# Channel attention: the bounds of the scores made from the queries' signs by GpSimd and TensorE, the key scans read from PSUM, and the own queries' work moved by a step

## The reference

```
Q = (x @ Wq + bq).reshape(b, s, H, C) * inv_sqrt_c      # H = 16 heads, C = 64 channels
K = (x @ Wk + bk).reshape(b, s, H, C)
V = (x @ Wv + bv).reshape(b, s, H, C)
scores = jnp.einsum('bshq,bshk->bshqk', Q, K)           # an outer product of 64 queries and 64 keys
scores = jnp.where(triu(ones((C, C)), 1), -inf, scores)  # channel q sees the keys 0..q
w = jax.nn.softmax(scores, axis=-1)
attn = jnp.einsum('bshqk,bshk->bshq', w, V).reshape(b, s, HID) @ Wo + bo
```

## Time and profile before

| | |
|---|---|
| median of 3 runs | 3225.54 us (3220.49 to 3230.01) |
| the profiled execution's own time | 3221.55 us |
| its span, first to last instruction | 3217.70 us |
| busy: TensorE / VectorE / ScalarE / GpSimd | 2606.6 / 2244.1 / 1852.5 / 1556.9 us |
| granted TensorE clock, mean | 0.946 |
| first scans of the four batches of the channel stage | 1525.29, 1927.99, 2330.64, 2733.28 us |
| exponentials of the own queries (L1660) | 2048, in all 708.2 us |

### The profile page before, as it was taken

One profiled execution on the slowest core, in us unless ns is written; L12 is line 12 of the kernel. 1 busy time (PEld: TensorE's weight loads), 2 busy tenths in 40 slices (PEclk: granted clock), 3 DMA queues, 4 the chain that ended last, 5 costly groups with the idle time before them and its releaser, 6 DMA issues. The chain is left out here.

```text
span 3217.7 us, 52070 instructions
## 1 busy us (share of the span) xinstructions
PE 2606.6 (81%) x19172; PEld 2068.6 (64%) x19172; DVE 2244.1 (70%) x4214; ACT 1852.5 (58%) x4363; POOL 1556.9 (48%) x1473
## 2 busy tenths in 40 slices
PE   1998799889987998777688876888768887688867
PEld 0465556555655565577577766777667776677757
DVE  2167516751675168523999969999699996999964
ACT  0364536453645355422877748777487774877743
POOL 0141314131413142312987729877298772987725
PEclk8999999989998999888999998999989999899988
DMA  9400000000000000075000000000000000000005
GB/s 239 130 2 1 5 10 2 1 5 10 2 1 5 10 2 1 18 274 185 4 8 1 1 4 4 7 1 1 4 4 7 1 1 4 4 7 1 1 28 161
DMA packets 75363, 93.12 MB, mean 29 GB/s; under 512 B 9325, under 2 KB 61340, under 8 KB 74985
## 3 DMA queue, kind: packets, MB, share of 16 engines
q1 hardware_dynamic: 24388, 51.54, 4.9%
q10 hardware_dynamic: 45540, 27.93, 3.6%
q0 software_dynamic: 5184, 10.29, 1.0%
HBM read 61.58 MB, written 28.62 MB: 28 GB/s over the span
## 5 line engine op out<-in xcount | busy, mean ns | idle before, releaser
L1701 POOL TENSOR_TENSOR arena<-arena 128x1536 f32<-128x1536 f32 (+9 forms) x480 | 1035.7, 2185 | 293.1 <-DVE arena L1765 247.7
L1569 PE MATMUL psum<-ident,arena 128*128 128x128 f32 (+7 forms) x7168 | 880.6, 282 | 293.3 <-ACT arena L1670 286.2
L1569 PEld LDWEIGHTS psum<-ident,arena 128*128 128x128 f32 (+7 forms) x7168 | 806.9, 139 | 397.5 <-ACT arena L1670 351.1
L1660 ACT ACTIVATE arena<-arena 128x64 f32<-128x64 f32 (+7 forms) x2048 | 708.2, 485 | 122.0 <-PE psum L1578 122.0
L1765 DVE TENSOR_TENSOR arena<-arena,psum 128x1536 f32<-128x1536 f32 (+9 forms) x480 | 494.7, 1064 | 52.8 <-ACT arena L1670 45.1
L1670 ACT ACTIVATE arena<-arena 128x1536 f32<-128x1536 f32 (+2 forms) x288 | 406.7, 1416 | 177.5 <-DVE arena L1751 177.5
L901 POOL TENSOR_SCALAR arena<-arena 128x512 f32<-128x512 f32 (+3 forms) x512 | 263.9, 532 | 498.5 <-DVE arena L864 498.3
L1751 DVE TENSOR_TENSOR arena<-arena,psum 128x1536 f32<-128x1536 f32 (+9 forms) x480 | 493.8, 1063 | 14.3 <-POOL arena L1701 12.5
L822 ACT ACTIVATE arena<-arena 128x512 f32<-128x512 f32 (+3 forms) x512 | 281.8, 552 | 183.2 <-DVE arena L857 183.2
L518 POOL TENSOR_SCALAR veps<-mv 128x1 f32<-128x1 f32 x112 | 21.5, 192 | 615.2 <-DVE mv L513 610.5
L775 PEld LDWEIGHTS psum<-ident,arena 128*128 128x128 f32 x1280 | 142.4, 145 | 169.9 <-ACT arena L833 84.7
(11 more groups left out here) (274 smaller groups left out, 3619.2 us busy)
## 6 DMA issues: line engine op xcount, KB each, us to landing
arena<-in_L_ffn_W SPq DMA_DIRECT2D x39, 768.0 KB
arena<-in_L_ffn_W SPq DMA_DIRECT2D x23, 514.0 KB
rows_d<-xrow ACTq DMA_DIRECT2D x1, 9504.0 KB, 51.0
y_d<-xrow ACTq DMA_DIRECT2D x1, 9216.0 KB
arena<-rows_d SPq DMA_DIRECT2D x62, 66.0 KB
y_d<-arena POOLq DMA_DIRECT2D x39, 64.0 KB
arena<-in_L_ffn_h_w ACTq DMA_DIRECT2D x2, 1024.0 KB
wa<-in_L_attn_W_attn ACTq DMA_DIRECT2D x1, 1536.0 KB
```

The lines of the kernel that those rows point to most:

```text
L1569: last = nc.tensor.matmul(ps[ch.half][0:rows, to:to + P], buf[:, c:c + rows], ident[:], start=first, stop=False, is_transpose=True, skip_g ...
L1660: nc.scalar.activation(by_key[:, 0:HD - r, j], keys[:, h, 0:HD - r], ACT.Exp, bias=NB[:, j:j + 1], scale=Q3[tt % 2][:, j:j + 1]).then_inc( ...
L1701: last = nc.gpsimd.tensor_tensor(of_piece(D3[n % 5], piece), q, keys_on(K3[tt % 2], k, nk, w), ALU.mult)
```

## The change

- Ahead of the tiles a matrix `minus` (the negative identity) is made once.
- `move_qk` also writes the queries' positive and negative parts (`QS`, two Relu, one with scale -1) for each half, and the keys by head a second time, into `psK`, the PSUM banks 5 and 6. The two scans read psK instead of KH, at step 11 instead of 12. The banks of psD are swapped.
- `maxima` is gone from VectorE, and ScalarE's copy of the queries into psM too. GpSimd multiplies the positive part by the maxima and the negative part by the minima (`times_pool`, four products of 128x512 a tile, and NB), at its steps 16 and 0; TensorE subtracts the one from the other into psM with two matmuls (`bound_pe`), at step 14 for one half and step 0 for the other.
- The own queries' shares lie in steps 2 to 13; their denominators' sums in steps 14 and 15, their weighing in 15 and 16, their numerators' sums in 16 and 17, ahead of the V fill of step 17.
- At a batch's start GpSimd does this behind the products of the chunks 0 and 1.

```diff
-        psD = [psum[:, 6, :], psum[:, 7, :]]
+        psD = [psum[:, 7, :], psum[:, 6, :]]
+        psK = psum[:, 5:7, :].rearrange("p a n -> p (a n)")
...
-        Q0_AT, MAX_0, FINISH_0, V1_AT = NC - 1, 0, 3, 3
+        FINISH_0, V1_AT = 3, 3
...
-        SCAN, MAX_1 = EARLY + 6, EARLY + 8
+        SCAN, TIMES_1, BOUND_1 = EARLY + 5, NC - 2, NC - 4
+        TIMES_0, BOUND_0 = 0, 0
...
-        OWN_STEPS = range(1, NC - 3)
+        OWN_STEPS = range(2, NC - 4)
...
-        OWN_DEN = {NC - 3: (0, 1), NC - 2: (2, 3)}
-        OWN_W = {NC - 2: (0, 1), NC - 1: (2, 3)}
-        OWN_NUM = {NC - 1: (0, 1), 0: (2, 3)}
+        OWN_DEN = {NC - 4: (0, 1), NC - 3: (2, 3)}
+        OWN_W = {NC - 3: (0, 1), NC - 2: (2, 3)}
+        OWN_NUM = {NC - 2: (0, 1), NC - 1: (2, 3)}
...
+        def bound_pe(pe, tt, half):
+            pe.wait_ge(c3["mq"], 2 * tt + 2 - half)
+            if half == 0 and tt > 0:
+                pe.wait_ge(c3["d"], tt * NC)
+            nc.tensor.matmul(psM[half], ident[:], MQ[half][0], start=True, stop=False)
+            nc.tensor.matmul(psM[half], minus[:], MQ[half][1], start=False, stop=True).then_inc(c3["m"], 1)
...
+                if j >= 2:
+                    if tt > 0:
+                        act.wait_ge(s["mq"], 2 * tt + 2 - j)
+                    for to, sign in zip(QS[j - 2], (1.0, -1.0)):
+                        nc.scalar.activation(to, qk_bank(tt, j), ACT.Relu, scale=sign)
...
                 if j < 2:
-                    by_head = KH[tt % 2].rearrange("p (h c) -> p c h", h=NH)[:, j * HD // 2:(j + 1) * HD // 2, :]
-                    nc.scalar.activation(by_head, qk_bank(tt, j).rearrange("p (c h) -> p c h", h=NH), ACT.Copy, scale=HD ** -0.5)\
-                        .then_inc(s["kh"], 1)
+                    if tt > 0:
+                        act.wait_ge(s["attn"], 2 * tt - 1)
+                    for to in (KH[tt % 2], psK):
+                        by_head = to.rearrange("p (h c) -> p c h", h=NH)[:, j * HD // 2:(j + 1) * HD // 2, :]
+                        last = nc.scalar.activation(by_head, qk_bank(tt, j).rearrange("p (c h) -> p c h", h=NH), ACT.Copy,
+                                                    scale=HD ** -0.5)
+                    last.then_inc(s["kh"], 1)
...
-                if c == Q0_AT and tt + 1 < NT:
-                    act.wait_ge(s["qk_sb"], 4 * tt + 8)
-                    act.wait_ge(s["d"], (tt + 1) * NC)
-                    nc.scalar.activation(psM[0], Q3[(tt + 1) % 2][:, 0:HB_], ACT.Copy).then_inc(s["q_ps"], 1)
...
+        def times_pool(pool, tt, half):
+            s = c3
+            pool.wait_ge(s["scan"], tt + 1)
+            pool.wait_ge(s["qk_sb"], 4 * tt + 4)
+            if tt > 0:
+                pool.wait_ge(s["m"], 2 * tt - half)
+            r = slice(half * HD // 2, (half + 1) * HD // 2)
+            for to, q, a in zip(MQ[half], QS[half], (PMX, PMN)):
+                keys = a.rearrange("p (h c) -> p c h", h=NH)[:, ::-1, :][:, r, :]
+                last = nc.gpsimd.tensor_tensor(to.rearrange("p (c h) -> p c h", h=NH),
+                                               q.rearrange("p (c h) -> p c h", h=NH), keys, ALU.mult)
+            last.then_inc(s["mq"], 1)
+            if half == 0:
+                pool.wait_ge(s["mq"], 2 * tt + 2)
+                if tt > 0:
+                    pool.wait_ge(s["own"], tt * len(own))
+                nc.gpsimd.tensor_tensor(NB, MQ[0][1][:, 0:NH * OWN], MQ[0][0][:, 0:NH * OWN], ALU.subtract).then_inc(s["neg"], 1)
...
                 for dst, f, op in ((PMX, first[0], ALU.max), (PMN, first[1], ALU.min)):
-                    last = nc.vector.tensor_tensor_scan(dst, f[:], KH[tt % 2], 0.0, ALU.add, op)
-                then(last)
-
-            def maxima(tt, half):
...
-                nc.vector.tensor_tensor(low, m, mn, ALU.mult)
-                then(nc.vector.tensor_tensor(m, m, mx, ALU.mult))
-                then(nc.vector.tensor_tensor(psM[half], psM[half], QN, ALU.max))
...
-                    nc.vector.tensor_scalar(NB, psM[0][:, 0:NH * OWN], -1.0, None, ALU.mult).then_inc(s["neg"], 1)
+                    last = nc.vector.tensor_tensor_scan(dst, f[:], psK, 0.0, ALU.add, op)
+                last.then_inc(s["scan"], 1)
```

More of the change, by code:

```diff
@@ L81, in transformer @@
         ustrict = sb("ustrict", P)
+        minus = sb("minus", P)
         ones = sb("ones", P)
@@ L134, in transformer @@
         gb, xb = wq1, wk1
+        QS = [[wa2[:, (2 * half + j) * T:(2 * half + j + 1) * T] for j in range(2)] for half in range(2)]
+        MQ = [[wa2[:, (4 + j) * T:(5 + j) * T] for j in range(2)], [wo1[:, j * T:(j + 1) * T] for j in range(2)]]
         rows_d = nc.dram_tensor("rows_d", ((NE + 1) * REGION, ROW), FP32, kind="Internal").ap()
@@ L225, in transformer @@
         KH = [take(NH * HD) for _ in range(2)]
-        QN = take(NH * HD // 2)
-        RD = QN
+        RD = take(NH * HD // 2)
         AT = [take(NH * HD) for _ in range(2)]
@@ L485, in transformer @@
             "d", "e", "w", "den", "num", "attn", "proj", "qk", "qk_sb", "v", "kh", "prod", "chain", "rows",
-            "own", "own_den", "own_w", "own_num", "q_ps", "neg")}
+            "own", "own_den", "own_w", "own_num", "scan", "mq", "m", "neg")}
         def x_ready(eng, stage):
@@ L1363, in experts2_dve @@
             fold_bias_dve(dve)
+            nc.vector.tensor_scalar(minus[:], ident[:], -1.0, None, ALU.mult)
             table_dve(dve, then, BLOCKS_2)
@@ L1525, in qk_bank @@
         def qk_bank(tt, j):
-            return psum[:, (4, 5, 3, 2)[j], :] if tt == 0 else scratch
+            return psum[:, (4, 7, 3, 2)[j], :] if tt == 0 else scratch
         def fill_qk(pe, tt, j):
@@ L1588, in channel_pe @@
             pe.wait_ge(s["kh"], 2)
-            idle_work(6, 24)
+            idle_work(4, 24)
+            bound_pe(pe, 0, 1)
+            bound_pe(pe, 0, 0)
             for n in range(NALL + 1):
@@ L1592, in channel_pe @@
                 if n < NALL:
+                    if c == 0:
+                        pe.wait_ge(s["scan"], tt + 1)
                     if tt > 0 and c == 0:
@@ L1605, in channel_pe @@
                         sum_own(psD, o).then_inc(s["own_den"], 1)
[L1606 to L1610, removed]
                 if n == NALL:
                     break
+                for o in OWN_NUM.get(c, ()):
+                    pe.wait_ge(s["own_w"], tt * PARTS + o + 1)
+                    sum_own(psA, o).then_inc(s["own_num"], 1)
+                if c == BOUND_0 and tt > 0:
+                    bound_pe(pe, tt, 0)
+                if c == BOUND_1 and tt + 1 < NT:
+                    bound_pe(pe, tt + 1, 1)
                 if c == V1_AT:
@@ L1693, in channel_pool @@
                     rstd_pool(pool, 1, tt - 1, tt - 1)
+                if n == 2:
+                    times_pool(pool, 0, 1)
+                    times_pool(pool, 0, 0)
+                if c == TIMES_0 and tt > 0:
+                    times_pool(pool, tt, 0)
+                if c == TIMES_1 and tt + 1 < NT:
+                    times_pool(pool, tt + 1, 1)
                 if n >= 5:
@@ L1722, in scan_keys @@
                 dve.wait_ge(s["kh"], 2 * tt + 2)
+                if tt > 0:
+                    dve.wait_ge(s["mq"], 2 * tt)
                 for dst, f, op in ((PMX, first[0], ALU.max), (PMN, first[1], ALU.min)):
-                    last = nc.vector.tensor_tensor_scan(dst, f[:], KH[tt % 2], 0.0, ALU.add, op)
-                then(last)
-            def maxima(tt, half):
[L1730 to L1736, removed]
-                nc.vector.tensor_tensor(low, m, mn, ALU.mult)
-                then(nc.vector.tensor_tensor(m, m, mx, ALU.mult))
-                then(nc.vector.tensor_tensor(psM[half], psM[half], QN, ALU.max))
-                if half == 0:
-                    if tt > 0:
-                        dve.wait_ge(s["own"], tt * len(own))
-                    nc.vector.tensor_scalar(NB, psM[0][:, 0:NH * OWN], -1.0, None, ALU.mult).then_inc(s["neg"], 1)
+                    last = nc.vector.tensor_tensor_scan(dst, f[:], psK, 0.0, ALU.add, op)
+                last.then_inc(s["scan"], 1)
             def subtract(n):
-                ch = chunks[n % NC]
+                tt, c = n // NC, n % NC
+                ch = chunks[c]
                 dve.wait_ge(s["prod"], n + 1)
+                if c == 0:
+                    dve.wait_ge(s["m"], 2 * tt + 1)
+                if c == EARLY:
+                    dve.wait_ge(s["m"], 2 * tt + 2)
                 for piece in ch.pieces:
@@ L1789, in channel_dve @@
             scan_keys(0)
-            maxima(0, 1)
-            maxima(0, 0)
             subtract(0)
@@ L1796, in channel_dve @@
                 if tt > 0:
-                    if c == MAX_0:
-                        maxima(tt, 0)
                     if c == FINISH_0:
@@ L1807, in channel_dve @@
                     finish(tt, 1)
[L1808 to L1812, removed]
+                if c == SCAN and tt + 1 < NT:
+                    scan_keys(tt + 1)
```

## The result

The changed kernel takes 3293.59 us (median of 4 runs, 3290.51 to 3295.59) against 3227.34 of before: the ratio is 1.0209, interval 1.0194 to 1.0224, so 2% slower. The forecast was 3291.

What follows compares the result with a forecast made beforehand. The prediction took a closed ScalarE-TensorE loop through the single buffer EA, 91.27 us a tile, as the bound. Batch start plus tile growth, 17.4 us a batch, 70 in four, on 3221.55 gave 3291, range 3245 to 3310.

Steps and rivals of the forecast that it cites:

- The loop is what sets the tile: ScalarE's own work and TensorE's own sums wait on each other through single-buffered EA: 64.09 + 1.53 + 25.65 = 91.27 us.
- ScalarE +0.26: ScalarE's stretch of own work: -2.76 exponentials, -0.66 gap, +1.92 Relu, +1.76 psK copies, in us a tile.
- 1.8 of waits: ScalarE waits 1.2 and 0.6 us for subtractions 3 and 5, late behind the V fill, in tiles 1 to 3.
- the gap that I had let go: ScalarE's single idle gap of 0.66 us in the own work's stretch, which the forecast took to disappear.
- TensorE +1.48: TensorE's tail to the last own sums: +0.44 chunk sums, -0.86 V fill, +1.9 bound matmuls, in us a tile.
- A tile's growth: Added time in a batch's tiles: 1.7 us in tile 0, 3.5 and 3.5 next, 1.7 in the last.
- The start, 7.0: At each batch's start, GpSimd's products and TensorE's bound make the own work 7.0 us late; bounds 4 to 11.
- The sum, 17.4 a batch: Start and tiles together, 7.0 + 1.7 + 3.5 + 3.5 + 1.7 us; four batches give 70 us.
- Scans at 2.29 beside GpSimd: VectorE's scans with keys in PSUM run at 2.29 us beside GpSimd; otherwise the start is 3.0 longer.
- Rival A: VectorE sets the tile, so 7.8 us less in 16 tiles makes it faster, 3113 or part of that; chance 0.08.
- B: No change: ScalarE's gaps and V's wait don't come, start costs 4 or less, 3222 to 3231; chance 0.06.
- C: GpSimd becomes late, its new products costing 3.3 us each: 16 to 30 us on top, 3307 to 3321; chance 0.08.

Runs made afterwards that it cites:

- e1: Kernel before, VectorE's three bound passes a half left out in tiles 1 to 3 of each batch, nothing added: 3214.36 us, ratio 0.9959.
- e6: Changed kernel without the four Relu of a tile's moves in tiles 1 to 3 of each batch: 3267.20 us, ratio 1.0129 to the kernel before.
- e8: Changed kernel with the next tile's early-half bound at the end of TensorE's step 12 instead of step 14: 3272.98 us, ratio 1.0152 to the kernel before.
- e4: Kernel before with only the shift of the own queries' work (shares in steps 2 to 13, sums and weighing sooner): 3236.26 us, ratio 1.0026.
- e2: Kernel before with TensorE's own-query sums ahead in its order, no instruction added or removed: 3190.97 us, ratio 0.9883.
- e7: Changed kernel with step 17's V fill ahead of the last own sums instead of behind them: 3288.31 us, ratio 1.0196 to the kernel before.
- e5: Changed kernel with the own queries' work put back where it was (shares in steps 1 to 14): 3274.44 us, ratio 1.0148 to the kernel before.
- e9: Changed kernel with the bounds of each batch's first tile made by VectorE, as before the change: 3277.50 us, ratio 1.0169 to the kernel before.

## Why the prediction was right, step by step

- **The loop is what sets the tile**: right for what it was used for. e1 (69 us off VectorE give 13), e6 and e8 (work on the loop is paid in full, or vanishes when moved off it) show it. But the loop and VectorE lie closer than the text said: in e4 the loop was shortened and the tiles stayed as long as they were, as VectorE took its place, and in e2 it took it after 8.3 us a batch. The rows had it: 88.28 of 91.27 busy. The change lengthened the loop and relieved VectorE, the one case in which this doesn't show.
- **ScalarE +0.26, and 1.8 of waits**: 66.16 - 64.09 is 2.07, the sum of the two nearly to the point, with errors that cancel. The stretch has 1.93 of idle time (0.93, 0.54, and 0.46 for TensorE's fill) where it had 0.66, so +1.27, and +0.80 of the rest, where -2.76 + 1.92 + 1.76 = +0.92 was forecast. The psK copy holds ScalarE 0.62 (2526.93 to 2527.55), not 0.88. Against that, the gap that I had let go came back as 0.46, since TensorE's 24 sums ahead of that fill took 5.18 us at a granted clock of 0.50 (the windows at the end show it) instead of 2.67 at 1.00 (the same sums in e1); and a wait costs more than the idle time shown, as instructions overlap otherwise: a share of 11 holds ScalarE 3.64 (2495.76 to 2499.40) and 4.33 ahead of the wait of 0.54 (2500.78 to 2505.11).
- **TensorE +1.48**: 26.95 - 25.65 = 1.30; the two matmuls held it 1.73, not 1.9.
- **Waits behind the late V fill, 1.8 a tile**: 1.47. The late V fill was named as the cause of both; e7 shows that without it the first goes and the second stays.
- **A tile's growth**: 1.7, 3.5, 3.5 were forecast, 1.14, 3.37 and 2.46 came; tile 2 grew by less than tile 1 in part because it has no gap of 0.46; the rest of that stays open. The stretch from the last own work's start to the next batch's first scan grew by 3.8 (111.10 to 114.91), of which 1.0 are the new psK copies. The rest was forecast at 1.7 and is 2.8, through a term that the prediction did not have: 1.7 us for the sums of step 14 at a granted clock of 0.61 (e5).
- **The start, 7.0**: 6.4 from the scan, 7.45 with the psK copies ahead of it (1.0 instead of 1.7). Luck has a part in it. A product of GpSimd with reversed, strided keys takes 1.5 us instead of 1.23, and the first bound took TensorE 3.7 us instead of 2.0, so the first subtraction came 17.0 us behind the scan instead of 14.7. The own work was only 1.1 later than forecast (23.68 against 22.6): VectorE's three subtractions ran without a gap (5.27) and did not wait for GpSimd's product of chunk 2, as the sum had it. e9 shows the start to be on the path.
- **The sum, 17.4 a batch**: 7.45 + 1.14 + 3.37 + 2.46 + 2.8 = 17.2. The mechanism holds, and no term of the sum is off by more than 1.1; that the sum is met within 0.2 is luck, since they are off in both directions. So is part of 3291: it started from a profiled execution 5.8 us under the median of the kernel before.
- **Scans at 2.29 beside GpSimd**: 2.26 to 2.29 in all 32, with GpSimd's products unhindered (those of two chunks, three instructions, in 7.00 from 2535.65).
- **Rival A** (VectorE as the bound) is out by e1; it would be right on the opened loop, by e2. **B** and **C** did not come: in the tiles GpSimd was in time, at 76.45 busy of 94.64, and VectorE never waited for it in tile 1; at 1.5 us its products cost half of the 3.3 of rival C.

## What to carry to other kernels

Follow a wait on a single buffer round until it closes, over all engines, before counting busy shares; work between two points of that loop is paid in full, work beside it only when something overtakes. Then ask of the busiest engine beside it by how much it trails, in both directions: that says how much the loop can lose as well as gain. When an experiment gives something, look in its trace where the time went before crediting it to the work that was left out: of e1's 2.9 us in its third batch, 1.6 were two gaps of ScalarE behind TensorE's slow sums. And where an engine works without a gap, order its queue by who waits: kernels above that differ only in that order differ by up to 1.2% (e2).

## What the runs showed of the hardware that was not expected

- TensorE's granted clock falls inside the stage, and where it does decides what it costs. At a batch's start two fp32 matmuls of 512 columns took 3.7 us at a granted clock of 0.50 (1.2 GHz), behind a gap of 7.43 us, and 1.73 us at 1.00 (2.4 GHz) in the tile. In tile 1 24 sums took 5.18 us at 0.50, behind a gap of 3.23 us, and held ScalarE up for 0.46. In the last tile of each batch 24 sums took 4.34 us at a mean of 0.61, behind a gap of 2.12 us, on the path (e5). The windows of the changed kernel:

```profile
2386.79:2390.50 3.71, 3.71 (x5) 1.59 (x6) 0.00 (x0) 0.00 (x0) 3.63 (x4) 0.50 0.00 0
2563.00:2566.00 3.00, 3.00 (x18) 2.00 (x17) 3.00 (x2) 0.00 (x0) 3.00 (x3) 1.00 0.00 0
2539.62:2544.80 5.18, 5.17 (x24) 5.18 (x25) 4.42 (x3) 5.18 (x14) 3.03 (x2) 0.50 0.00 0
2738.97:2743.31 4.34, 4.34 (x25) 4.31 (x25) 2.85 (x3) 3.53 (x3) 0.00 (x0) 0.61 0.01 4
```

- ScalarE writes a strided copy of 128x512 into PSUM in 695 ns and into SBUF in 1071, both out of PSUM, while contiguous ones take 583 (L1674, SBUF to PSUM) and 594 (L1642, PSUM to SBUF) in the kernel before. The groups by form (busy us, mean ns):

```profile
L1678 ACT ACTIVATE arena<-psum 128x512 f32<-128x512 f32 x32 | 34.3, 1071 | 0.0
L1678 ACT ACTIVATE psum<-psum 128x512 f32<-128x512 f32 x32 | 22.2, 695 | 0.0
```

The Trainium skill, "ScalarE: Activation LUTs" (section "Step-by-step: what each stage is for"), has PSUM as the faster destination: for the strided form these rows agree; the contiguous pair differs by 11 ns and reads from different memories.
- A VectorE scan of 1024 with one input in PSUM takes 2.26 to 2.29 us, alone or beside GpSimd's products; with both in SBUF 2.28 to 4.4 in the kernel before, and up to 4.9 in e2. The Trainium skill's rule in "SBUF — State Buffer" (section "SBUF: two separate sides"), that a VectorE instruction with two SBUF inputs and a GpSimd one exclude each other, agrees with these times.
